# Mamba scan of a three-stage kernel: dt and u spread by broadcast DMA reads, drives on GpSimd, decay in PSUM, half-row scans

## The reference, cut to what matters

```python
xh, z = jnp.split(x @ W_in, 2, axis=-1)
xh = silu(causal_conv_k2(xh, conv_w, conv_b))
x_dbl = xh @ W_x                                  # dt_low (4), B (16), C (16)
dt = softplus(dt_low @ W_dt + b_dt)               # 128 channels
A = -exp(A_log)                                   # 128 x 16
def step(h, inp):                                 # over the 1024 tokens
    dt_t, B_t, C_t, x_t = inp
    dA = exp(dt_t[..., None] * A)
    dBx = dt_t[..., None] * B_t[:, None, :] * x_t[..., None]
    h = dA * h + dBx
    return h, einsum('bdn,bn->bd', h, C_t)
y = (scan + xh * D) * silu(z);  return y @ W_out
```

## Time and profile before

| | |
|---|---|
| runs | 1614.7, 1634.39, 1636.29 us, median 1634.39 |
| the profiled execution's own time | 1626.1 us |
| its span from first to last instruction | 1624.0 us |
| mean granted clock of TensorE, full speed = 1 | 0.761 |
| busiest engines | PE 1260.7 us, DVE 1171.9, ACT 704.3, GpSimd (POOL) 512.2 |
| instructions | 17597 |
| DMA on SP's queue | 53.73 MB, 14.6% of 16 engines' span |

### The profile page before, as it was taken

The page is one execution under the profiler, slowest core; times in us unless marked ns, Lnnn a source line. Parts: engine busy times, 40 slices in busy tenths (PEclk is TensorE's granted clock), DMA queues, the critical chain, the costliest instruction groups (busy, mean ns, idle before and its releaser), DMA issues. The chain is left out here.

```text
span 1624.0 us, 17597 instructions
## 1 busy us (share of the span) xinstructions
PE 1260.7 (78%) x6388; PEld 499.9 (31%) x6388; DVE 1171.9 (72%) x1388; ACT 704.3 (43%) x1298; POOL 512.2 (32%) x272
## 2 busy tenths in 40 slices
PE   2455346888888987888887987888888988899894
PEld 1111111323233333333333323333233324433433
DVE  3396398787678968887679867887688867348345
ACT  1423322347434762376335642476326631460470
POOL 2454454344334332342243333342144321000000
PEclk9567556659966998589867997599758985695696
DMA  1100320021202111201211120201220120020000
GB/s 38 45 1 13 83 53 13 7 68 30 55 8 68 30 32 38 67 1 30 62 29 45 30 50 19 68 10 23 47 61 14 30 49 17 19 51 21 3 14 7
DMA packets 25863, 54.87 MB, mean 34 GB/s; under 512 B 8531, under 2 KB 8919, under 8 KB 23448
## 3 DMA queue, kind: packets, MB, share of 16 engines
q1 hardware_dynamic: 25776, 53.73, 14.6%
HBM read 28.15 MB, written 12.98 MB: 25 GB/s over the span
## 5 line engine op out<-in xcount | busy, mean ns | idle before, releaser
L926 DVE TENSOR_REDUCE row_max<-ps 128x1 f32<-128x768 f32 (+7 forms) x384 | 355.9, 952 | 142.2 <-PE ps L1202 139.6
L660 POOL TENSOR_TENSOR read<-state,c_rep 128x1024 f32<-128x1024 f32 x128 | 303.9, 2374 | 466.2 <-DVE state L970 450.6
L801 ACT ACTIVATE probs<-ps 128x512 f32<-128x512 f32 (+3 forms) x768 | 329.5, 496 | 144.7 <-PE ps L1305 86.5
L970 DVE TENSOR_TENSOR_SCAN state<-decay,drive 128x1024 f32<-128x1024 f32 x128 | 357.1, 2790 | 1.8 <-POOL read L660 1.1
L1198 PE MATMUL ps<-k_stack,q_stack 72*128 72x512 bf16 (+3 forms) x768 | 280.6, 456 | 83.2 <-DVE row_max L926 64.3
L1302 PE MATMUL ps<-q_stack,k_stack 75*128 75x512 bf16 (+3 forms) x768 | 222.8, 353 | 32.7 <-DVE drive L979 17.8
L979 DVE TENSOR_TENSOR drive<-ps,b_rep 128x512 f32<-128x512 f32 x256 | 169.6, 676 | 105.7 <-PE ps L1236 105.0
L762 ACT ACTIVATE decay<-ps,a_scale 128x512 f32<-128x512 f32 x256 | 175.3, 696 | 116.8 <-DVE state L970 100.1
L1236 PE MATMUL ps<-dt_rows,pick 96*128 96x512 bf16 x256 | 120.5, 471 | 96.9 <-DVE drive L979 69.5
L1317 PE MATMUL ps<-probs,v_aug 128*32 128x512 f32 (+3 forms) x1536 | 177.4, 536 | 4.1 <-ACT acc_sb L790 1.6
L1198 PEld LDWEIGHTS ps<-k_stack,q_stack 72*128 72x128 bf16 x768 | 73.8, 116 | 274.2 <-DVE row_max L926 171.4
(11 more groups left out here) (169 smaller groups left out, 1281.6 us busy)
## 6 DMA issues: line engine op xcount, KB each, us to landing
q_stack<-q_parts_dram SPq DMA_DIRECT2D x48, 192.0 KB
k_stack<-k_parts_dram SPq DMA_DIRECT2D x48, 192.0 KB
dt_rows<-read SPq DMA_DIRECT2D x96, 64.0 KB, 2.0
u_rows<-read SPq DMA_DIRECT2D x96, 64.0 KB, 2.0
k_parts_dram<-read SPq DMA_DIRECT2D x40, 128.0 KB, 2.4
q_parts_dram<-read SPq DMA_DIRECT2D x24, 128.0 KB, 2.3
xs<-in_x SPq DMA_DIRECT2D x8, 256.0 KB, 3.5
residual<-in_x SPq DMA_DIRECT2D x8, 256.0 KB, 9.6
```

The source lines that it names most:

```text
L660: pool.tensor_tensor(read[:, k % (2 * NG), :], state[:, k % 2, :], c_rep[:, :], ALU.mult)\
L801: act.activation(probs[:, e % (2 * QUAD), 0:w], bank_of(("scores", e))[:, 0:w], ACT.Exp, scale=SCALE).then_inc(exped.sem, 1)
L926: dve.tensor_reduce(row_max[:, i, h0:h0 + nh], scores[:, :, 0:P * (i + 1)], AX.X, ALU.max, negate=True).then_inc(row_maxed.sem, 1)
L970: dve.tensor_tensor_scan(state[:, k % 2, :], decay[:, k % 2, :], drive[:, k % 3, :], 0.0, ALU.mult, ALU.add).then_inc(scanned.sem, 1)
```

## The change

- dt and u are stored whole to DRAM in float32 (`dt_dram`, `u_dram`), and for each unit a DMA reads 8 rows of 512 tokens 16 times over, straight into a [128, 512] slot in SBUF. There are 6 slots for dt and 8 for u, so 64 loads of 256 KB for each image take the place of 24 DMAs of 64 KB. The three-part split (4 casts on ACT, 4 differences on GpSimd) and PE's 64 spreading matmuls go.
- The drive u*B moves from DVE to GpSimd, now from SBUF, 6 units ahead of the read multiplication, which also goes by half chunks.
- ACT computes decay from the SBUF slot into PSUM (banks 0 and 1 in turn).
- DVE scans 512 tokens at a time: each chunk's second half follows the first at once and takes its last state as the start.
- `RING` shrinks from five banks to three (5, 6, 7). Three of f's tiles get banks 2 and 3. Folds do both halves at once: three fold rounds in the rounds, one in the next front.
- On SP the first 8 u loads and 6 dt loads stand in the front, the others are in the rounds behind the store and read of the maxima, with the reads of the next image's q and k (6 from unit 22 on, 6 behind all units) in the same queue.

```diff
-        decay = sb("decay", [P, 2, T])
-        drive = sb("drive", [P, 3, T])
-        state = sb("state", [P, 2, T])
-        read = sb("read", [P, 2 * NG, T])
+        DT_SLOTS, U_SLOTS, DRIVE_SLOTS, STATE_SLOTS, READ_SLOTS = 6, 8, 8, 4, 12
-        UNITS_IN = (2, 2, 2, 1, 0, 2, 2, 0, 2, 1, 2, 1, 1, 1, 2, 1, 0, 0, 1, 1, 2, 1, 1, 2, 0, 1, 0, 1)
-        FOLDS = ((0, 0, 13), (0, 1, 13), (1, 0, 18), (1, 1, 19))
+        UNITS_IN = (2, 2, 1, 1, 1, 1, 1, 1, 1, 1, 2, 1, 1, 1, 1, 1, 1, 1, 1, 1, 1, 1, 2, 1, 1, 1, 1, 1)
+        FOLDS = ((0, 8), (1, 15), (2, 22))
+        TURN_BANK = {("attn_t", 0): 3, ("attn_t", 1): 2, ("proj", 0): 3}
+        STACKS_AT = 22
+        DRIVES_AHEAD = 6
-        RING = (0, 1, 5, 6, 7)
+        DECAY = (0, 1)
+        RING = (5, 6, 7)
@@ sync
+                    def load_rows(u, rows, slots, arrived):
+                        h, _, j = unit_of(u)
+                        slot = nth(c, u) % slots
+                        src = (dt_dram if rows is dt_rep else u_dram)[c.number, j * CH:(j + 1) * CH, halves(h)]
+                        sp.dma_start(rows[:, slot, :], src.unsqueeze(0).to_broadcast([NS, CH, BANK]))\
+                          .then_inc(arrived[slot].sem, 16)
+                        for n in range(U_SLOTS):
+                            load_u(n)
+                        for n in range(DT_SLOTS):
+                            load_dt(n)
...
+                    for n in range(UNITS):
+                        if c and n + U_SLOTS < UNITS:
+                            load_u(n + U_SLOTS)
+                        if c and n + DT_SLOTS < UNITS:
+                            load_dt(n + DT_SLOTS)
+                        if p and 0 <= n - STACKS_AT < 6:
+                            load_stack(0, n - STACKS_AT)
@@ gpsimd
-                    for k in range(NJ):
-                            pool.wait_ge(scanned.sem, scanned.at(c, k + 1))
-                            pool.tensor_tensor(read[:, k % (2 * NG), :], state[:, k % 2, :], c_rep[:, :], ALU.mult)\
+                    def drive_unit(u):
+                        pool.wait_ge(u_in[nth(c, u) % U_SLOTS].sem, landed(c, u, U_SLOTS))
+                        if u >= DRIVE_SLOTS:
+                            pool.wait_ge(scanned.sem, scanned.at(c, u - DRIVE_SLOTS + 1))
+                        pool.tensor_tensor(drive[:, u % DRIVE_SLOTS, :], u_rep[:, nth(c, u) % U_SLOTS, :],
+                                           b_rep[:, halves(h)], ALU.mult).then_inc(driven.sem, 1)
+                    for u in range(UNITS):
+                            if u + DRIVES_AHEAD < UNITS:
+                                drive_unit(u + DRIVES_AHEAD)
+                            read_unit(u)
@@ scalar
-                        act.activation(decay[:, k % 2, halves(h)], bank_of(("dt", k2)), ACT.Exp,
+                        if u >= 2:
+                            act.wait_ge(scanned.sem, scanned.at(c, u - 1))
+                        act.wait_ge(dt_in[slot].sem, landed(c, u, DT_SLOTS))
+                        act.activation(banks(DECAY[u % 2]), dt_rep[:, slot, :], ACT.Exp,
@@ vector
-                        dve.tensor_tensor_scan(state[:, k % 2, :], decay[:, k % 2, :], drive[:, k % 3, :], 0.0,
-                        dve.tensor_tensor(drive[:, k % 3, halves(h)], bank_of(("u", k2)), b_rep[:, halves(h)],
+                        if u >= STATE_SLOTS:
+                            dve.wait_ge(read_out.sem, read_out.at(c, u - STATE_SLOTS + 1))
+                        if h:
+                            dve.wait_ge(scanned.sem, scanned.at(c, u))
+                        carry = state[:, (u - 1) % STATE_SLOTS, BANK - 1:BANK]
+                        dve.tensor_tensor_scan(state[:, u % STATE_SLOTS, :], banks(DECAY[u % 2]),
+                                               drive[:, u % DRIVE_SLOTS, :], carry if h else 0.0,
+                                               ALU.mult, ALU.add).then_inc(scanned.sem, 1)
```

More of the change, by code:

```diff
@@ L304, in _ @@
                 diagonal(ident_bf[:, :], [[-1, P]], 0)
-                then(pool.memset(pick[:, :, :, :], 0.0))
-                for part_row in range(3):
-                    diagonal(pick[:, :, :, :], [[-CH, JG], [0, NS], [-1, CH]], -32 * part_row)
                 then(pool.memset(mask_q[:, :], 0.0))
@@ L480, in ring_users @@
                 if at_step:
[L481 to L485 removed]
+                    users += [("scores", QUAD * s + hq) for hq in range(QUAD)]
                     if s - LAG in LAST_STEP:
                         users.append(("heads", LAST_STEP.index(s - LAG)))
[L488 to L489 removed]
                 if f:
[L491 removed]
+                    users += [turn for turn in turns if turn not in TURN_BANK]
             if b:
@@ L1231, in turn_maxima @@
                         last.then_inc(max_t_ps.sem, 1)
-                    def replicate(k2, bank, rows):
-                        g, q, _ = chunk(k2 // 2)
-                        return pe.matmul(bank, pick[:, q, :, :].rearrange("p n e -> p (n e)"),
-                                         rows[:, g, halves(k2 % 2)], start=True, stop=True)
                     places = ring_places(c, b, f)
@@ L1338, in program @@
                             weigh(s, range(QUAD - 1))
-                        if c and units:
-                            unit(units[0])
                         if b and n == 0:
```

300 lines of the change are left out of this document (143 added, 157 removed).

## The result

The kernel after takes 1693.14 us in the median of 3 runs (1690.02 to 1700.05), against 1634.39 before: the ratio is 1.0395 with a 95% interval of 1.0289 to 1.0502. The forecast was 1536 us (range 1485 to 1600) and faster. It is slower, and outside the range. In the medians and ratios of this document a run over 1.5% above the fastest of the same kernel isn't counted; this concerns one run of one kernel.

The account below looks back on a forecast made before the run. It took DVE's queue (scans and drives) to bound the full trips' rounds. Terms: -90 full trips, -4 trip 3, -14 trips 1 and 2, +10 trips 9 and 10, -98 in all: 1626.1 to 1528, median 1536 us, range 1485 to 1600.

Parts of the forecast that it names:

- 0.2 us in 24 rounds is 5 us a trip: Trips 9 and 10: with three banks PE waits for an exponential each round, +10 us for both trips.
- decays leave the ring too, so that each round has four users or five in place of more than six: Argument on ring users per round, against a rival in which three banks cost eight trips 8 us more each.
- The ring of three starves ACT: Rival: each of the eight trips with exponentials loses 8 us more, 1600 us in all; chance 0.07.
- Two paths of 76.5 and 80.5 that wait for one another in order ... don't end before the later: I take 83: Full trips' rounds: GpSimd ends at 76.5, PE and ACT at 80.5; five trips' rounds go from 505 to 415, -90 us.
- GpSimd ... ends at 76.5: Full trips' rounds: from 10 us on, 54 products of 1.20 us, 64.8, and an inverse root of 1.6.
- GpSimd becomes the wall: Rival: GpSimd's work grows from 38 to about 78 us a full trip; at 1.35 a product, 1603 to 1610 us; chance 0.11.
- Trips 1 and 2: First scan at 61 where it was 67.7, then 56 GpSimd instructions in 67 us against 71: -14 us for both.
- the first dt load is issued at 56.1 and lands at 59.3: Trip 1: 8 u loads at 0.6 us each are issued ahead of it; the first scan follows at 61.
- The scan lost its contention: DVE's scans: with decay in PSUM, GpSimd's reads no longer lengthen them; 1.21 us for 512 tokens, 38.8 for 32.
- The loads are hidden: Rounds: 64 loads of 256 KB a trip costed at nothing; the rival that they aren't hidden gave about 1752 us, chance 0.10.
- GpSimd's pause before drive 8: Trips with b: GpSimd waits some 4 us for u load 8, queued on SP behind the maxima's store and read.

Follow-up runs that it names:

- e3: Kernel after, with decay still in PSUM but as one more user of a ring of five banks: 1616.37 us, ratio 0.991 to the kernel before.
- e1: Kernel after, with five ring banks only in trips without a scan (9, 10 and 11), three elsewhere: 1666.2 us, ratio 1.020 to the kernel before.
- h3: Kernel before, with its ring cut to banks 5, 6 and 7 for all users, nothing else changed: 1724.15 us beside 1630.92.
- e6: e3 with GpSimd's drives and reads after the first image on 128 of 512 tokens, output not the reference's: 1588.39 us.
- e4: Kernel after, with each spread load after the first image moving 32 of its 512 tokens, output not the reference's: 1690.12 us.
- g8: e3 with all drives back on DVE, from SBUF: 1590.92 us in the median of three, ratio 0.9754 to the kernel before.
- e2: Kernel after, with decay in a pair of SBUF slots instead of PSUM banks 0 and 1, and a ring of five banks everywhere: 1774.24 us.
- g3: e3 with the drives split, first halves of a chunk on GpSimd and second halves on DVE: 1614.49 us, ratio 0.9895 to the kernel before.

## Why the prediction was wrong

The forecast missed by 157 us (1693 less 1536). Giving the ring its five banks back takes 77 of them away (e3); the other 80 remain with five banks. So two steps failed.

**The step that made the kernel slower: "0.2 us in 24 rounds is 5 us a trip".** The ring was priced at +10 us for trips 9 and 10 together and at nothing for the other trips. With the clock that went with it, it cost 77 us between the medians (84 between the spans, of which 53 in the full trips' rounds and 23 in trips 9 and 10). The price was worked out as a mean wait for an exponential. Measured, three banks cost 13 us in each of trips 9 and 10 (69.7 against 56.8), and e1 gives 10.5 and 12 of them back. With three banks PE's weight loads wait 23.6 us for exponentials in trip 9's rounds (43 waits, the longest 2.5), before 16.7 (27, the longest 1.7). These 7 us are only half of the 13. The mean left out the single stalls: a slow reader of one tile (DVE's expert product behind the gate's operations) now stops PE within two tiles, as the 4.31 us at 743.26 show in a full trip.

**"decays leave the ring too, so that each round has four users or five in place of more than six".** This argument against the rival failed. It counts users per round, but trips 9 and 10 have no decays to take away, and there the loss of two banks in five adds 10 us by itself (h3). The rival "The ring of three starves ACT", at 8 us more for each of eight trips, was the nearest to what happened, and had a chance of 0.07. For trips 9 and 10 it was right: 5 and 8 are the 13 measured. On full trips the ring's part is 5 us at a like clock and 10 to 12 in most with the lower clock. The 1600 us of the rival were still far too low, because of the next step.

**"Two paths of 76.5 and 80.5 that wait for one another in order ... don't end before the later: I take 83".** This is the larger error, and the ring isn't all of it. With five banks the rounds are 99.7, with GpSimd's work light 95.3, with drives on DVE 98.6; five rounds of e3 are 501 us together, the forecast had 415, and these 86 us cover the 80 that remain. The busy times of ACT and GpSimd were forecast rightly (ACT 61.6 behind the first exponential, measured 58 to 59). DVE's was forecast at 63 for the rounds and is 69.6. PE's was forecast at 61 there; with five banks and a clock of 0.90 it is 65, and in the kernel after, at 0.77 to 0.87, 71 to 80. But an engine that is busy 64 to 75 us in such a chain of four doesn't run at 90%. The waits of e3 form a circle: PE waits for a bank, the bank for a scan, the scan for a decay, the decay for exponentials ahead of it in ACT's queue, and these for PE. Before, DVE's queue was the slow one (busy 85 of 102 us, idle 0.1 us before its scans), and the others waited mostly for it. Afterwards no engine is that busy, and delays are passed on. The forecast had 2.5 us for this coupling (83 less 80.5). Over the 80.5 the runs show 15 (95.3, e6) to 19 (e3). That it is the circle of waits and nothing else is argued from these waits; no run takes the circle apart.

**The clock.** The forecast took PE's cost from rows at 0.89 to 0.93. The granted clock in the full trips' rounds after is 0.74 to 0.83. PE lost the 64 spreading matmuls, 26.5 us in a full trip's rounds: the 13.3 of those for dt and the 13.2 of those for u, whose line in 678 to 780 of the trace before is

```profile
L1236 PE MATMUL ps<-u_rows,pick 96*128 96x512 bf16 x31 | 13.2, 425 | 3.1 <-DVE attn L996 1.4 <-DVE moe L1061 0.9 <-DVE drive L979 0.6
```

Yet its busy time went from 88.1 to 89.9. Its three fold rounds have 9.7 us (forecast 6.2), the scores' matmuls alone went from 28.6 to 34.2. In one run of one program the same instructions took 112.1 us at 0.74 and 105.9 at 0.83; e1 and e4 show the same two lengths in other trips (112.4 at 0.76 and 106.0 at 0.84; 111.0 at 0.78 and 105.8 at 0.81), and trip 9 has 90.3 and 84.1 without any scan. So some 6 us of a full trip come with the clock. Why it falls stays open: that PE idles more is only argued, and h3 has long waits at 0.88.

**"GpSimd ... ends at 76.5".** Here the mechanism was right and the size off by little. In the rounds 58 instructions are busy 73 us (the forecast had 66.4 for 55 of them, from 10 us on), and the product's price is 1.27 to 1.29, between the bounds. "GpSimd becomes the wall" didn't happen in full trips: it waits 37.5 us for scans. But in trips 1 and 2 it was the wall, as stated, and there GpSimd was busy 67.9 of 71 us in 56 instructions, with no wait ahead of a drive. By the Trainium skill (GPSIMD Engine Reference, section Elementwise — side-by-side cycle accounting) an addition of two tensors of 2048 elements takes 4497 ns on GpSimd, and elementwise work is for DVE as a rule. The prediction has a product in place of the addition. A quarter of the figure is an estimate of 1.12 us, and the trace has 1.27 for a product. The measurement decides on the size, and g8 bears the rule out: with the drives on DVE the kernel is faster.

**Trips 1 and 2.** Forecast -14, measured -5.8. "the first dt load is issued at 56.1 and lands at 59.3": it was issued at 57.49, and ACT began behind it at 64.41. Eight u loads are on their way ahead of it. A load landed 3.2 us later in a quiet stretch; in this burst dt loads took 7.3 us in the median (44 to 70 us). ACT then loads its table for 1.28 us before the first decay, which the forecast left out. The first scan started at 66.43, forecast 61. The scans themselves then took 67.8 and 69.3 us in the two trips, where they took 71.0 and 71.7 and the forecast had 67.

**What was right.** The scan lost its contention: 1.196 to 1.225 us, as against 2.269 to 4.315 for twice the tokens. The Trainium skill (SBUF — State Buffer, section Who interferes with whom) has it that a DVE instruction with at most one SBUF input, outside the modes that use both ports, doesn't contend with GpSimd. The trace agrees (1.225 us at most), and e2 shows the other half at 2.1 us. The loads are hidden in the rounds of the kernel after (e4), at 3.6 and 4.5 us from issue to landing. GpSimd's pause before drive 8 was forecast at some 4 us and is this row of its order of time:

```profile
700.00 1.26 POOL L658 TENSOR_TENSOR drive<-u_rep,b_rep 128x512 f32<-128x512 f32 x1 [4.12 <-DMA u_rep<-u_dram]
```

**What stays open.** How the last 12 us (95.3 against 83) divide between the coupling, PE's clock, late loads and the order of the users; no full trip with the change's work had a clock over 0.87. Why the clock differs between trips of one program. And what the fronts' 12 us are.

## What to carry to other kernels

Count the buffers of a shared ring as a resource of the path that sets the end: price a smaller ring by the slowest reader of a single tile, not by the mean wait, and try it by itself first (one line in the kernel before shows at least 10 us a trip). When a change takes the slowest engine out of a chain of four, don't expect the next one's busy time over 90%: here 75 to 78 us of work in the busiest engine gave 95 to 100. And in a shared ring, a buffer that is filled by one engine and freed by another, two steps on, isn't to be filled early. Last, compare stretches at a like granted clock before a difference is put down to an edit: 6 us of 106 to 112 came and went with it.

## What the runs showed of the hardware

- DVE instructions other than scans met GpSimd too. With GpSimd busy 73 us of a full trip's rounds, two layer-norm operations with both inputs in SBUF took 1.71 and 1.69 us, where before they took 0.69 and 0.66 (and in e6, with GpSimd light, 0.96 and 0.67). DVE's work beside the scans was 29.5 us (69.55 less 40.0) against 22.4 (84.7 less 62.3), a part of it by where the stretch begins. Groups by line in trip 5's rounds, after:

```profile
L927 DVE TENSOR_TENSOR xcen<-t,ln_s 128x512 f32<-128x512 f32 x1 | 1.7, 1708 | 0.0
L505 DVE TENSOR_TENSOR xn<-xcen,ln_s 128x512 f32<-128x512 f32 x1 | 1.7, 1691 | 0.0
```

- The other way round as well: GpSimd's read was 1.27 us beside DVE scans from PSUM, and 1.46 in the mean where DVE made the drives from SBUF (g8), 1.39 where it made half of them (g3).
- An ACT exponential of 512 tokens costs 0.70 us from SBUF to PSUM, as from PSUM to SBUF.
- The granted clock of like stretches within one execution lay between 0.74 and 0.83, with 8.6 us between PE's busy times for the same matmuls. At an unchanged clock (0.93 and 0.94), 398 matmuls were busy 54.8 us with five banks and 59.3 with three.
